# A transformer block on one core: a new order for the head's embedding, three units and the last MLP

## The chip, the core and the metric
## What is computed
Four sequences of 512 tokens pass an embedding, an attention with 32 query heads on 8 key/value heads, and an MLP of 16 small heads. The embedding sums, over 8 shards of the table, the row of a token clipped into the shard. All shards but one give an edge row (their first or last), so the sum is one gathered row plus edge rows with coefficients.
```python
for shard in 8 shards: acc = acc + W[clip(x - start, 0, 1574)]
h = acc + 8 * bias + pos_emb                      # (4, 512, 1024)
a = layernorm(h)
q, k, v = split(a @ w_qkv.T)                      # 32 and 8 and 8 heads of 128
h = h + softmax(causal(q k^T / sqrt(128))) v @ w_dense.T
t = layernorm(h)[..., perm]                       # 16 heads of 64
t = gelu(t @ up[head]) @ down[head]               # 64 -> 256 -> 64
out = h + t[..., unperm]
```

## The kernel before
All work is cut into steps of a kind, a sequence `b`, a group `g` (one key/value head with its four query heads) and an index. `schedule()` lays the steps out in one list from orders written out by hand as strings; every engine walks the same list and does its part of each step. So a token's place in a string is its place in each engine's queue at once. There are a START, then per sequence eight units of about 81 us: unit 0 is FIRST or STATS, unit 1 of later sequences is MLP0, units 2 to 4 MID or MLP, then GATHER, EMBED and TURN, which prepare the next sequence; the last sequence ends with LAST and REST and then the "end" steps, the last sequence's MLP.

The tokens that matter here:
- `A`, `G`, `J`: positions loaded, table rows gathered, and (first sequence) positions added to them. `B0` to `B7`: the edge rows' sum for one half of one block of 128 tokens, with VectorE's statistics. `La`, `Lb`: root of the variance, shift, and ScalarE's normalising of the block. `X0` to `X7`: the normalised block is transposed by TensorE, copied as its high part by ScalarE (L717), and its low part (`xn_lo`, L885) made by VectorE.
- `Q`, `K`, `V`: projections of 24 matmuls in fp32r high/low parts. `S`: scores. `E`: four exponentials on ScalarE; where an order has no `E` token, `unit()` puts the E step directly behind its S. `N`: normalised probabilities, `Ta`/`Tb`: their transposes, `PV`: values, `D`: one of eight dense outputs, added into `hacc` (L830). `H`: the transposed residual. `Z`, `Y`: statistics of the second layernorm and their spreading over partitions. `F`, `P`, `U`, `O`: gather, normalise, up and down projection of a pair of MLP heads, "end F/P/U/O" the same for the last sequence.

Steps of kinds Q, K, V, D, H, Z, Y, B, X, O and end O are jobs. A job writes one of two PSUM banks `fb` in turn, and waits until the job two before it has been read out:
```python
def bank(s):
    return job[s] % 2
def start_job(s):
    if before(s) > 0:
        pe.wait_ge(bank_free[bank(s)], before(s))
```
An X bank is free after L885, a Q bank after L813 (`q_lo`), an H or Y bank after ScalarE's copy (L688, L693), a D bank after L830. Q0 of a new sequence also waits for X7. Weight tiles are loaded four ahead by SyncE (L385), rounded by ScalarE (L633, `split`) and given their low part by GpSimd (L927, `low`); the list `splits` says at which step. Eleven tiles are kept.

At the start VectorE turns the edge rows (0/1 coefficients L748) into three bf16 parts by L762 to L767: one cast and one subtraction of all 96 partitions, then casts and a subtraction of 32.

Of the kernel before, what the change touches and what calls it, by code (L numbers as in the profile page):

```python
# [14 lines left out]
P = 128  # L15
# [34 lines left out]

FIRST = ("S0 N0 Q2 H0 Ta0 H1 Tb0 H2 S1 H3 E1 N1 Q3 H4 Ta1 PV0 Tb1 H5 S2 H6 E2 N2 H7 Q0 Ta2 PV1 Tb2 S3 K N3 Q1 Ta3 PV2 "
         "Tb3 V PV3 VT")
# [3 lines left out]
         "Q1 Ta3 Z5 PV2 Z6 Tb3 V Z7 PV3 VT")  # L57
MLP0 = ("S0 N0 Q2 Y0 Ta0 H0 Y1 Tb0 f H1 S1 H2 E1 N1 Q3 H3 Ta1 D0 Tb1 H4 S2 H5 E2 p F D1 H6 D2 N2 H7 D3 D4 D5 D6 D7 u0 "
        "u1 PV0 u2 u3 Ta2 Q0 Tb2 S3 P N3 PV1 o K U0 U1 Ta3 PV2 U2 U3 Q1 Tb3 V PV3 VT")
# [5 lines left out]
         "PV1 K N3 Q1 Ta3 PV2 Tb3 V PV3 VT")  # L65
TURN = ("S0 N0 Q2 D0 Ta0 La4 D1 Tb0 S1 N1 Lb4 Q3 Ta1 X0 D2 Tb1 X1 S2 D3 D4 N2 X2 D5 X3 D6 X4 D7 X5 PV0 X6 Ta2 X7 Tb2 S3 "
        "PV1 Q0 N3 K Q1 Ta3 PV2 Tb3 V PV3 VT")
LAST = ("S0 N0 Q2 D0 Ta0 D1 Tb0 S1 N1 Q3 W D2 Ta1 PV0 Tb1 S2 D3 D4 N2 D5 Ta2 PV1 Tb2 S3 D6 N3 D7 PV2 Ta3 d0 Tb3 d1 "
        "PV3")
START = ("A G0 G1 G2 G3 J0 J1 J2 J3 B0 B1 La0 B2 Lb0 B3 La1 B4 Lb1 X0 X1 B5 La2 B6 Lb2 X2 X3 B7 La3 Lb3 X4 X5 X6 X7 "  # L70
         "Q0 K Q1 V VT")
# [41 lines left out]
def schedule():  # L113
    steps = unit(START, -1, 7)
    for b in range(B):
        steps += unit(STATS if b else FIRST, b, 0)
        for g in range(1, 5):
            steps += unit((MLP0 if g == 1 else MLP) if b else MID, b, g)
        if b + 1 < B:
            steps += unit(GATHER, b, 5) + unit(EMBED, b, 6) + unit(TURN, b, 7)  # L120
        else:
            steps += [s for s in unit(GATHER, b, 5) if s.kind not in ("A", "G")] + unit(MID, b, 6) + unit(LAST, b, 7)
    steps += unit(REST, B, 0)

    end = lambda kind, i: [Step("end " + kind, B - 1, 0, i)]
    for p in range(PAIRS):
        steps += end("F", p)
    for p in range(PAIRS):
        steps += end("P", p) + end("U", 4 * p) + end("U", 4 * p + 1)
        if p > 0:  # L130
            steps += end("O", p - 1)
        steps += end("U", 4 * p + 2) + end("U", 4 * p + 3)
    return steps + end("O", PAIRS - 1)
# [6 lines left out]
class Tally:  # L140

    def __init__(self):
        jobs = [s for s in STEPS if s.kind in JOBS]
        self.at = {s: n for n, s in enumerate(STEPS)}
# [18 lines left out]
        for m in range(RW):  # L164
            first = Step("X", 0, 0, min(m // 2 * 2 + 1, 7)) if m < 8 else Step("Q", 0, 0, 0)
            self.splits[first].append(m)
# [12 lines left out]
def tower_kernel(nc, x_cols, x_row, table, bias, pos, edge_cols, w_qkv, w_dense, w_mlp, perm_cols, out):  # L179
# [28 lines left out]
    with ctx:  # L208
        def sb(name, shape, dt, at=ctx):
            return at.enter_context(nc.sbuf_tensor(name, shape, dt))  # L210
# [68 lines left out]
        row_sum = sb("row_sum", [P, TT], F32)  # L279
        inv_sum = sb("inv_sum", [P, TT], F32)  # L280

# [28 lines left out]
        gathered = [sem(f"gathered{c}") for c in range(TT)]  # L311
        h_placed = sem("h_placed")
        h_stats = sem("h_stats")
        h_moments = sem("h_moments")
# [46 lines left out]
        def up_bank(s):  # L361
# [3 lines left out]
            return (sc[:, 0, :], sc[:, 1, :], sc[:, 2, :], tp[:, 0, :], tp[:, 1, :], pv[:, :])[s.i % 6]  # L365

        def heads_of(s):

            return (end_at_hi, end_at_lo) if (s.b, s.g) == (B - 1, G - 1) else (at_hi, at_lo)
# [12 lines left out]
        def _(sp):  # L382
# [13 lines left out]
            for part in range(3):  # L396
                at = slice(32 * part, 32 * part + 32)
                sp.dma_start(edge_consts[at, :], edge_cols).then_inc(const_in, 16)
                token_row(at, 0, S, const_in)
            positions(first_pos)  # L400
            for m in range(RAW):
# [31 lines left out]
        def _(pe):  # L433
# [80 lines left out]
            for s in STEPS:  # L514
# [46 lines left out]
                elif s.kind == "H":  # L561
                    half, c = s.i // 4, s.i % 4
                    if s.i == 0:
                        pe.wait_ge(*free(Step("B", s.b, 0, 7)))
                    four(start_job(s), lambda j: h_tok[:, c, (4 * half + j) * P:(4 * half + j + 1) * P])
                elif s.kind == "Z":
# [9 lines left out]
                elif s.kind == "B":  # L576
# [3 lines left out]
                    if s.b == 1 and s.i == 0:  # L580
                        pe.wait_ge(coef_rest, 1)
                    dst = start_job(s)
                    mm = pe.matmul(dst, coef[:, s.b * S + c * P:s.b * S + (c + 1) * P],
                                   edges[:, half * S:(half + 1) * S], start=True, stop=s.b > 0)
                    if s.b == 0:
                        pe.wait_ge(h_placed, c + 1)
                        mm = pe.matmul(dst, ident[:, :], h_tok[:, c, half * S:(half + 1) * S], start=False, stop=True)
                    mm.then_inc(job_full, 1)
                elif s.kind == "X":
# [29 lines left out]
        def _(act):  # L619
# [5 lines left out]
            for part in range(3):  # L625
                at = 32 * part
                act.dma_start(row_buf[at:at + n, :], shards[0:n, VS - 1, :]).then_inc(edge_in, 16)
                act.dma_start(row_buf[at + n:at + 2 * n, :], shards[1:SHARDS, 0, :]).then_inc(edge_in, 16)
                act.dma_start(row_buf[at + 2 * n:at + EDGE, :], bias.partition_broadcast(SHARDS)).then_inc(edge_in, 16)

            def split(m):
# [11 lines left out]
            for s in STEPS:  # L643
# [47 lines left out]
                elif s.kind == "Y":  # L691
                    act.wait_ge(job_full, full(s))
                    act.activation((rstd2 if s.i else mean2)[:, :], fb[:, bank(s), :], copy)\  # L693
                       .then_inc(bank_free[bank(s)], 1)
                elif s.kind == "Z" and s.i == 7:
                    act.wait_ge(stat_step, 6 * s.b + 6)
                    act.activation(root2[:, :], inv_var2[:, :], ACT.Sqrt).then_inc(root_done, 1)
                elif s.kind == "B" and s.b == 0:
                    c, half = s.i // 2, s.i % 2

                    act.wait_ge(h_stats, s.i + 1)
                    act.activation(h_tok[:, c, half * S:(half + 1) * S], fb[:, bank(s), :], copy)\
                       .then_inc(bank_free[bank(s)], 1)
                elif s.kind == "La":
# [3 lines left out]
                elif s.kind == "Lb":  # L708
                    act.wait_ge(shift_done, tally.la[Step("La", *s[1:])] + 1)
                    if s.b == 0:  # L710
                        act.wait_ge(*free(Step("B", 0, 0, 2 * s.i)))
                        act.wait_ge(*free(Step("B", 0, 0, 2 * s.i + 1)))
                    normalise_tokens(s.b, s.i % TT)
# [25 lines left out]
        def _(dve):  # L739
# [30 lines left out]
            for s in STEPS:  # L770
# [85 lines left out]
                elif s.kind == "B":  # L856
                    c, half = s.i // 2, s.i % 2
                    at = h_tok[:, c, half * S:(half + 1) * S]
                    if s.b > 0 and half == 0:
                        dve.wait_ge(gathered[c], 16 * s.b + 16)  # L860
                    dve.wait_ge(job_full, full(s))
                    if s.b > 0:
                        dve.tensor_tensor(at, at, fb[:, bank(s), :], ALU.add).then_inc(bank_free[bank(s)], 1)
                        dve.wait_ge(*free(s))
                    dve.bn_stats(stats[:, c, half, :], at if s.b > 0 else fb[:, bank(s), :]).then_inc(h_stats, 1)
                    if half == 1:
                        dve.wait_ge(h_stats, 8 * s.b + s.i + 1)
                        dve.bn_aggr(moments[:, c, :], stats[:, c, :, :]).then_inc(h_moments, 1)
                elif s.kind == "La":
                    cs = slice(s.i, s.i + 1) if s.i < TT else slice(0, TT)  # L870
# [28 lines left out]
                elif s.kind == "end P":  # L899
                    if s.i == 0:  # L900
                        dve.wait_ge(*free(Step("Y", s.b, 0, 1)))
                        dve.wait_ge(*free(Step("Y", s.b, 0, 0)))
                    at = end_y[:, s.i, :]
                    dve.wait_ge(end_turned[s.i], 16)
                    dve.tensor_tensor(at, end_rows[:, s.i, :], mean2[:, :], ALU.subtract).then_inc(end_centred, 1)
                    dve.wait_ge(end_centred, s.i + 1)
                    dve.tensor_tensor(at, at, rstd2[:, :], ALU.mult).then_inc(end_scaled, 1)
                elif s.kind == "end O":
                    at = end_rows[:, s.i, :]
                    dve.wait_ge(job_full, full(s))  # L910
                    dve.tensor_tensor(at, at, fb[:, bank(s), :], ALU.add).then_inc(bank_free[bank(s)], 1)
                elif s.kind == "O":
                    dve.wait_ge(job_full, full(s))
                    at = hp[:, s.i % 2, :]
                    dve.tensor_tensor(at, at, fb[:, bank(s), :], ALU.add).then_inc(bank_free[bank(s)], 1)

        @block.gpsimd
        def _(pool):
# [11 lines left out]
            for s in STEPS:  # L930
                if s.kind == "G":
# [5 lines left out]
                    else:  # L937
                        pool.wait_ge(pos_in[s.i], 16 * s.b + 16)
                        pool.indirect_dma_start(out=h_tok[:, s.i, :], out_offset=None, in_=table, in_offset=token,
                                                compute_op=ALU.add).then_inc(gathered[s.i], 16)  # L940
                elif s.kind == "J":
                    pool.wait_ge(pos_in[s.i], 16)
                    pool.wait_ge(gathered[s.i], 16)
                    pool.tensor_tensor(h_tok[:, s.i, :], h_tok[:, s.i, :], first_pos[:, s.i, :], ALU.add)\
                        .then_inc(h_placed, 1)
                elif s.kind == "end F":
# [88 lines left out]
```

## Time and profile before

| | |
|---|---|
| median of 3 runs | 2688.78 us (2688.01 to 2689.4) |
| the profiled execution: its own time | 2691.08 us |
| its span, first to last instruction | 2689.3 us |
| mean granted TensorE clock | 0.994 |
| TensorE, VectorE, ScalarE, GpSimd busy | 2603.3, 1247.8, 1233.7, 916.6 us |
| first Q0 starts | 54.84 us |
| last h_tok addition ends | 2679.2 us |

The profile is one execution. "Idle before, releaser" names what ended an engine's wait. Busy time of an engine that others don't wait for costs nothing, and the units between the head and the end repeat with a period of about 81 us.

### The profile page before, as it was taken

The page shows a single profiled execution, that of the slowest core. Times are in us where ns is not written, and L with a number is a line of the kernel's source. Part 1 is how long each engine was busy: PE and PEld are TensorE (multiplying, and loading weights), DVE is VectorE, ACT ScalarE, POOL GpSimd, SP SyncE. Part 2 cuts the span into 40 slices and gives each one's busy share as a digit, 9 for nine tenths or more (in the row PEclk, how much of TensorE's full clock was granted, in tenths as well). Part 3 has the DMA queues.
Part 4 walks back from the last instruction along what each step waited for, and adds up shares of the span by engine and source line. Part 5 has one row for each costly group of instructions (what it writes and reads, how often), then busy time and mean ns, then how long its engine had stood idle before and what let it go on. Part 6 is the DMA issues. An engine that isn't in the chain of part 4 may idle for free.

```text
span 2689.3 us, 35616 instructions
## 1 busy us (share of the span) xinstructions
PE 2603.3 (97%) x12864; PEld 2104.8 (78%) x12864; DVE 1247.8 (46%) x3110; ACT 1233.7 (46%) x3052; POOL 916.6 (34%) x730
## 2 busy tenths in 40 slices
PE   4999999999999999999999999999999999999996
PEld 2788888887877777888887877788888778778872
DVE  4444444454544444455454444446545344434443
ACT  3544444445454454445445454544544444454432
POOL 4333333332333333433233333343332233333312
PEclk8999999999999999999999999999999999999998
DMA  4222223322322222432222222252232222222222
GB/s 126 79 67 75 75 71 109 88 75 59 102 79 82 80 75 87 125 83 63 75 87 80 86 87 78 75 137 66 69 97 72 71 87 87 91 63 75 67 75 71
DMA packets 112129, 221.49 MB, mean 82 GB/s; under 512 B 13394, under 2 KB 13394, under 8 KB 111956
## 3 DMA queue, kind: packets, MB, share of 16 engines
q1 hardware_dynamic: 104400, 193.78, 24.3%
q0 software_dynamic: 7424, 25.17, 3.4%
q8 instruction: 104, 1.70, 0.3%
q14 instruction: 69, 0.57, 0.1%
q10 hardware_dynamic: 132, 0.27, 0.0%
HBM read 202.40 MB, written 16.78 MB: 81 GB/s over the span
## 4 chain that ended last, share of the span: by engine, by line
PE 91%; DVE 4%; ACT 3%; issue 1%; DMA 0%; ACTq 0%; POOL 0%; DVEq 0%
PE fb L435 22%; PE fb L437 21%; PE fb L436 21%; PE tp L456 4%; PE sc L435 2%; PE sc L436 2%; PE sc L437 2%; PE sc L499 2%; PE fb L508 2%; PE pv L435 2%; PE pv L437 2%; PE pv L436 2%; PE sc L447 1%; ACT w_hi L633 1%; PE fb L493 1%; PE pv L468 1%
## 5 line engine op out<-in xcount | busy, mean ns | idle before, releaser
L927 POOL TENSOR_TENSOR w_lo<-w_raw,w_hi 128x512 fp32r<-128x512 f32 x640 | 818.9, 1295 | 1595.2 <-ACT w_hi L633 1595.2
L435 PE MATMUL fb<-xn_hi,w_hi 128*128 128x512 f32 x1536 | 610.8, 398 | 3.4 <-DVE stats L835 1.7
L437 PE MATMUL fb<-xn_hi,w_lo 128*128 128x512 f32 x1536 | 601.6, 392 | 0.0
L436 PE MATMUL fb<-xn_lo,w_hi 128*128 128x512 f32 x1536 | 600.4, 391 | 0.0
L633 ACT ACTIVATE w_hi<-w_raw 128x512 fp32r<-128x512 f32 x640 | 382.6, 632 | 386.7 <-PE fb L437 383.4
L435 PE MATMUL fb<-at_hi,w_hi 128*128 128x512 f32 x992 | 394.8, 398 | 8.2 <-DVE hacc L830 6.1
L649 ACT ACTIVATE prob<-sc,neg_max 128x128 f32<-128x128 f32 (+3 forms) x512 | 262.9, 526 | 280.0 <-DVE neg_max L783 279.1
L437 PE MATMUL fb<-at_hi,w_lo 128*128 128x512 f32 x992 | 387.9, 391 | 0.0
L436 PE MATMUL fb<-at_lo,w_hi 128*128 128x512 f32 x992 | 387.2, 390 | 0.0
L435 PEld LDWEIGHTS fb<-xn_hi,w_hi 128*128 128x128 f32 x1536 | 289.4, 188 | 81.8 <-issue 18.8
L437 PEld LDWEIGHTS fb<-xn_hi,w_lo 128*128 128x128 f32 x1536 | 289.2, 188 | 61.9
L830 DVE TENSOR_TENSOR hacc<-hacc,fb 128x512 f32<-128x512 f32 x256 | 175.8, 687 | 344.7 <-PE fb L437 344.1
L436 PEld LDWEIGHTS fb<-xn_lo,w_hi 128*128 128x128 f32 x1536 | 289.6, 189 | 58.4
L780 DVE CUSTOM_DVE_ANT_0 sc<-sc,mask 128x128 f32<-128x128 f32 (+3 forms) x512 | 235.6, 521 | 1.0 <-PE sc L437 0.6
L791 DVE TENSOR_SCALAR prob<-prob,inv_sum 128x128 f32<-128x128 f32 (+3 forms) x512 | 230.2, 512 | 4.5
L435 PEld LDWEIGHTS fb<-at_hi,w_hi 128*128 128x128 f32 x992 | 186.4, 188 | 58.6 <-issue 22.3
L808 DVE TENSOR_TENSOR at_lo<-pv,at_hi 128x512 fp32r<-128x512 f32 x124 | 85.4, 689 | 287.2 <-ACT at_hi L664 287.2
L437 PEld LDWEIGHTS fb<-at_hi,w_lo 128*128 128x128 f32 x992 | 186.3, 188 | 39.7
L436 PEld LDWEIGHTS fb<-at_lo,w_hi 128*128 128x128 f32 x992 | 186.6, 188 | 36.4
L813 DVE TENSOR_TENSOR q_lo<-fb,q_hi 128x384 fp32r<-128x384 f32 x128 | 71.4, 558 | 299.5 <-ACT q_hi L672 299.0
L671 ACT ACTIVATE q_first<-fb 128x128 f32<-128x128 f32 x128 | 35.4, 277 | 371.9 <-PE fb L437 371.9
L456 PEld LDWEIGHTS tp<-ident,prob 128*128 128x128 f32 x1280 | 150.8, 140 | 62.9 <-issue 18.2
(142 smaller groups left out, 3457.6 us busy)
## 6 DMA issues: line engine op xcount, KB each, us to landing
w_raw<-in_w_qkv SPq DMA_DIRECT2D x384, 256.0 KB, 2.7
w_raw<-in_w_dense SPq DMA_DIRECT2D x256, 256.0 KB, 2.6
h_rows<-hacc SPq DMA_DIRECT2D x32, 256.0 KB, 2.4
h_tok<-in_pos SPq DMA_DIRECT2D x12, 512.0 KB, 6.0
mlp_w<-in_w_mlp SPq DMA_DIRECT2D x24, 256.0 KB, 3.0
first_pos<-in_pos SPq DMA_DIRECT2D x4, 512.0 KB, 10.2
end_w<-in_w_mlp SPq DMA_DIRECT2D x8, 256.0 KB, 4.0
hacc<-in_x_row SPq DMA_DIRECT2D x3, 192.0 KB, 13.9
```

Of the source, the lines that this page charges most:

```text
L435: pe.matmul(dst, a_hi, b_hi, start=first, stop=False)
L436: pe.matmul(dst, a_hi, b_lo, start=False, stop=False)
L437: return pe.matmul(dst, a_lo, b_hi, start=False, stop=last)
L456: return pe.transpose(tp[:, at, c:c + P], prob[:, P_OFF[t] + j * P:P_OFF[t] + (j + 1) * P], ident[:, :])
L633: act.activation(w_hi[:, m % RW, :], w_raw[:, m % RAW, :], copy).then_inc(w_rounded, 1)
L649: act.activation(prob[:, P_OFF[t]:P_OFF[t] + w], sc[:, at, c:c + w], ACT.Exp, bias=neg_max[:, t:t + 1], scale=SCALE, accum_out=row_sum[:, ...
L780: dve.tensor_tensor_reduce(one, one, mask[:, S - w:S], 1.0, LOWEST, ALU.add, ALU.max, row_max[:, t:t + 1]).then_inc(tile_max, 1)
L791: dve.tensor_scalar(at, at, inv_sum[:, t:t + 1], None, ALU.mult).then_inc(prob_ready, 1)
L808: dve.tensor_tensor(lo[:, s.i, :], pv[:, :], hi[:, s.i, :], ALU.subtract).then_inc(pv_free, 1)
L813: dve.tensor_tensor(lo, fb[:, bank(s), at], hi, ALU.subtract).then_inc(bank_free[bank(s)], 1)
L830: dve.tensor_tensor(hacc[:, s.i, :], hacc[:, s.i, :], fb[:, bank(s), :], ALU.add)\
L927: pool.tensor_tensor(w_lo[:, m % RW, :], w_raw[:, m % RAW, :], w_hi[:, m % RW, :], ALU.subtract)\
```

## The change
- Head: SyncE waits for the edge rows before it issues the loads of positions and weights. The positions are added by VectorE (step J), not GpSimd. The first sequence's B steps are no jobs any more: they use six banks that are idle then (`first_bank`), with semaphores of their own, `first_full` and `first_free`. START has a new order with each J in front of its pair of B's, and the first weight tiles are split at B0 to B3 and X1 to X6 in place of the X's and Q0.
- Table loads: ScalarE runs one-column activations (`warm`) with the root's or Gelu's function at the start, at Z0 and after the last root.
- MLP0: the H steps stand earlier. TURN: X2 stands behind S2, X3 to X7 behind D7, around PV0, Ta2, Tb2, S3 and PV1.
- End: `end P` of a pair stands one pair ahead, and the first waits for the two spread statistics one by one.
```diff
-MLP0 = ("S0 N0 Q2 Y0 Ta0 H0 Y1 Tb0 f H1 S1 H2 E1 N1 Q3 H3 Ta1 D0 Tb1 H4 S2 H5 E2 p F D1 H6 D2 N2 H7 D3 D4 D5 D6 D7 u0 "
+MLP0 = ("S0 N0 Q2 Y0 H0 Y1 H1 Ta0 H2 Tb0 f S1 H3 E1 N1 Q3 Ta1 H4 D0 Tb1 H5 S2 H6 H7 E2 p F D1 D2 N2 D3 D4 D5 D6 D7 u0 "
         "u1 PV0 u2 u3 Ta2 Q0 Tb2 S3 P N3 PV1 o K U0 U1 Ta3 PV2 U2 U3 Q1 Tb3 V PV3 VT")
-TURN = ("S0 N0 Q2 D0 Ta0 La4 D1 Tb0 S1 N1 Lb4 Q3 Ta1 X0 D2 Tb1 X1 S2 D3 D4 N2 X2 D5 X3 D6 X4 D7 X5 PV0 X6 Ta2 X7 Tb2 S3 "
-        "PV1 Q0 N3 K Q1 Ta3 PV2 Tb3 V PV3 VT")
+TURN = ("S0 N0 Q2 D0 Ta0 La4 D1 Tb0 S1 N1 Lb4 Q3 Ta1 X0 D2 Tb1 X1 S2 X2 D3 D4 N2 D5 D6 D7 X3 PV0 X4 X5 Ta2 Tb2 S3 X6 "
+        "X7 PV1 Q0 N3 K Q1 Ta3 PV2 Tb3 V PV3 VT")
-START = ("A G0 G1 G2 G3 J0 J1 J2 J3 B0 B1 La0 B2 Lb0 B3 La1 B4 Lb1 X0 X1 B5 La2 B6 Lb2 X2 X3 B7 La3 Lb3 X4 X5 X6 X7 "
+START = ("A G0 G1 G2 G3 J0 B0 B1 J1 La0 B2 B3 Lb0 J2 La1 X0 X1 Lb1 B4 B5 J3 La2 X2 X3 Lb2 B6 B7 La3 X4 X5 Lb3 X6 X7 "
          "Q0 K Q1 V VT")
...
+    steps += end("P", 0)
     for p in range(PAIRS):
-        steps += end("P", p) + end("U", 4 * p) + end("U", 4 * p + 1)
+        if p + 1 < PAIRS:
+            steps += end("P", p + 1)
+        steps += end("U", 4 * p) + end("U", 4 * p + 1)
...
-        jobs = [s for s in STEPS if s.kind in JOBS]
+        jobs = [s for s in STEPS if s.kind in JOBS and s[:2] != ("B", 0)]
...
-            first = Step("X", 0, 0, min(m // 2 * 2 + 1, 7)) if m < 8 else Step("Q", 0, 0, 0)
+            first = Step("B", 0, 0, m) if m < 4 else Step("X", 0, 0, m - 3) if m < 10 else Step("Q", 0, 0, 0)
...
+        def first_bank(i):
+
+            return (sc[:, 0, :], sc[:, 1, :], sc[:, 2, :], tp[:, 0, :], tp[:, 1, :], pv[:, :])[i % 6]
...
+
+            sp.wait_ge(edge_in, 144)
             positions(first_pos)
...
+                    if s.b == 0 and s.i > 5:
+                        pe.wait_ge(first_free, s.i - 5)
+                    dst = start_job(s) if s.b > 0 else first_bank(s.i)
...
+            act.wait_ge(zeroed, 4)
+            act.activation(warm[:, 0:1], ones[:, 0:1], ACT.Sqrt)
...
+                elif s.kind == "Z" and s.i == 0 and s.b == B - 1:
+                    act.activation(warm[:, 1:2], ones[:, 0:1], ACT.Sqrt)
                 elif s.kind == "Z" and s.i == 7:
                     act.wait_ge(stat_step, 6 * s.b + 6)
                     act.activation(root2[:, :], inv_var2[:, :], ACT.Sqrt).then_inc(root_done, 1)
+                    if s.b == B - 1:
+                        act.activation(warm[:, 2:3], ones[:, 0:1], ACT.Gelu)
...
+                elif s.kind == "J":
+                    dve.wait_ge(pos_in[s.i], 16)
+                    dve.wait_ge(gathered[s.i], 16)
+                    dve.tensor_tensor(h_tok[:, s.i, :], h_tok[:, s.i, :], first_pos[:, s.i, :], ALU.add)\
+                       .then_inc(h_placed, 1)
...
                 elif s.kind == "end P":
                     if s.i == 0:
-                        dve.wait_ge(*free(Step("Y", s.b, 0, 1)))
                         dve.wait_ge(*free(Step("Y", s.b, 0, 0)))
                     at = end_y[:, s.i, :]
                     dve.wait_ge(end_turned[s.i], 16)
                     dve.tensor_tensor(at, end_rows[:, s.i, :], mean2[:, :], ALU.subtract).then_inc(end_centred, 1)
+                    if s.i == 0:
+                        dve.wait_ge(*free(Step("Y", s.b, 0, 1)))
...
-                elif s.kind == "J":
-                    pool.wait_ge(pos_in[s.i], 16)
-                    pool.wait_ge(gathered[s.i], 16)
-                    pool.tensor_tensor(h_tok[:, s.i, :], h_tok[:, s.i, :], first_pos[:, s.i, :], ALU.add)\
-                        .then_inc(h_placed, 1)
```

## Rows read from the trace of the kernel before

**Rows 1.** The page: busy us, share of the span, instructions.
```profile
PE 2603.3 (97%) x12864; PEld 2104.8 (78%) x12864; DVE 1247.8 (46%) x3110; ACT 1233.7 (46%) x3052; POOL 916.6 (34%) x730
```
**Rows 2.** TensorE's waits, whole span: us in total, times, longest.
```profile
PE fb L583 <- DVE edges L767: 24.8, 1, 24.8
...
PE sc L499 <- DVE end_y L907: 6.5, 5, 2.2
```
**Rows 3.** Timeline, 11 to 25 us: start, us, engine, line, operation.
```profile
11.14 0.69 DVE L762 CAST edges<-row_buf 96x1024 bf16<-96x1024 f32 x1 [4.20 <-DMA row_buf<-in_bias]
11.87 1.22 DVE L763 TENSOR_TENSOR row_buf<-row_buf,edges 96x1024 f32<-96x1024 f32 x1
12.19 11.87 POOL L944 TENSOR_TENSOR h_tok<-h_tok,first_pos 128x1024 f32<-128x1024 f32 x4 [3.57 <-DMA h_tok<-in_table,rows]
...
18.61 3.24 DVE L766 TENSOR_TENSOR row_buf<-row_buf,edges 32x1024 f32<-32x1024 f32 x1
21.89 2.71 DVE L767 CAST edges<-row_buf 32x1024 bf16<-32x1024 f32 x1
```
**Rows 4.** DMA queues, 2 to 6 us, then 6 to 11.1: packets, MB, share.
```profile
q10 hardware_dynamic: 86, 0.18, 15.7%
...
q1 hardware_dynamic: 266, 0.98, 57.0%
q0 software_dynamic: 156, 0.59, 36.5%
q10 hardware_dynamic: 46, 0.09, 6.1%
```
**Rows 5.** The tile first_pos, its four loads.
```profile
DMA to landing us min/median/max: 7.2/10.2/13.3
```
**Rows 6.** The chain that ended last, in the head: start, us, what.
```profile
25.34 1.71 PE fb L587 x2
27.04 0.43 PE fb L583
...
46.21 0.87 PE fb L587 x2
```
**Rows 7.** Timeline, first matmul of Q0 in the first unit.
```profile
54.84 0.80 PE L435 MATMUL fb<-xn_hi,w_hi 128*128 128x512 f32 x1 [1.41 <-DVE xn_lo L885]
```
**Rows 8.** Windows: us, busy time; the granted clock is third or fourth from the end.
```profile
49.20:51.40 2.20, 0.00 (x0) 0.83 0.63 190
...
54.80:60.90 6.10, 6.06 (x14) 4.79 (x15) 0.00 (x0) 0.30 (x1) 2.37 (x2) 0.50 0.53 145
...
751.90:788.00 36.10, 33.81 (x176) 27.39 (x175) 21.27 (x64) 20.82 (x55) 11.14 (x9) 1.00 0.29 87
```
**Rows 9.** Timeline of the first TURN unit, 617 to 645 us.
```profile
617.14 1.24 ACT L640 ACTIVATE row_buf<-h_tok,shift,rstd 128x1024 f32<-128x1024 f32 x1
618.11 0.39 PE L435 MATMUL fb<-at_hi,w_hi 128*128 128x512 f32 x1
620.03 0.37 ACT L649 ACTIVATE prob<-sc,neg_max 128x128 f32<-128x128 f32 x1 [1.65 <-DVE neg_max L783]
622.05 0.64 ACT L633 ACTIVATE w_hi<-w_raw 128x512 fp32r<-128x512 f32 x1
644.11 0.47 PE L435 MATMUL fb<-xn_hi,w_hi 128*128 128x512 f32 x1
```
**Rows 10.** TensorE's waits, 595 to 660 us.
```profile
PE fb L435 <- DVE hacc L830: 1.2, 3, 0.4
PE tp L456 <- DVE pt_lo L795: 0.7, 1, 0.7
```
**Rows 11.** Timeline of the first MLP0 unit, 757 to 762 us.
```profile
759.69 0.55 DVE L813 TENSOR_TENSOR q_lo<-fb,q_hi 128x384 fp32r<-128x384 f32 x1
759.83 1.09 PE L456 MATMUL tp<-ident,prob 128*128 128x128 f32 x8 [1.29 <-DVE prob L791]
```
**Rows 12.** The chain that ended last, one pair of the last MLP.
```profile
2649.66 0.69 DVE h_tok L911
2650.35 0.61 DVE end_y L905
...
2650.99 0.70 DVE end_y L907
...
2651.73 1.13 PE sc L499 x4
2652.86 1.89 PE fb L508 x8
```

More of the change, by code:

```diff
@@ L280, in tower_kernel @@
         inv_sum = sb("inv_sum", [P, TT], F32)
+        warm = sb("warm", [P, 3], F32)
         with ExitStack() as own:
@@ L312, in tower_kernel @@
         h_placed = sem("h_placed")
+        first_full = sem("first_full")
+        first_free = sem("first_free")
         h_stats = sem("h_stats")
@@ L562, in _ @@
                     half, c = s.i // 4, s.i % 4
-                    if s.i == 0:
+                    if s.i == 0 and s.b > 0:
                         pe.wait_ge(*free(Step("B", s.b, 0, 7)))
+                    elif s.i == 0:
+                        pe.wait_ge(first_free, 8)
                     four(start_job(s), lambda j: h_tok[:, c, (4 * half + j) * P:(4 * half + j + 1) * P])
@@ L581, in _ @@
                         pe.wait_ge(coef_rest, 1)
-                    dst = start_job(s)
+                    if s.b == 0 and s.i > 5:
+                        pe.wait_ge(first_free, s.i - 5)
+                    dst = start_job(s) if s.b > 0 else first_bank(s.i)
                     mm = pe.matmul(dst, coef[:, s.b * S + c * P:s.b * S + (c + 1) * P],
@@ L587, in _ @@
                         mm = pe.matmul(dst, ident[:, :], h_tok[:, c, half * S:(half + 1) * S], start=False, stop=True)
-                    mm.then_inc(job_full, 1)
+                    mm.then_inc(job_full if s.b > 0 else first_full, 1)
                 elif s.kind == "X":
@@ L701, in _ @@
                     act.wait_ge(h_stats, s.i + 1)
-                    act.activation(h_tok[:, c, half * S:(half + 1) * S], fb[:, bank(s), :], copy)\
-                       .then_inc(bank_free[bank(s)], 1)
+                    act.activation(h_tok[:, c, half * S:(half + 1) * S], first_bank(s.i), copy)\
+                       .then_inc(first_free, 1)
                 elif s.kind == "La":
@@ L710, in _ @@
                     if s.b == 0:
-                        act.wait_ge(*free(Step("B", 0, 0, 2 * s.i)))
-                        act.wait_ge(*free(Step("B", 0, 0, 2 * s.i + 1)))
+                        act.wait_ge(first_free, 2 * s.i + 2)
                     normalise_tokens(s.b, s.i % TT)
@@ L860, in _ @@
                         dve.wait_ge(gathered[c], 16 * s.b + 16)
-                    dve.wait_ge(job_full, full(s))
+                    if s.b > 0:
+                        dve.wait_ge(job_full, full(s))
+                    else:
+                        dve.wait_ge(first_full, s.i + 1)
                     if s.b > 0:
@@ L864, in _ @@
                         dve.wait_ge(*free(s))
-                    dve.bn_stats(stats[:, c, half, :], at if s.b > 0 else fb[:, bank(s), :]).then_inc(h_stats, 1)
+                    dve.bn_stats(stats[:, c, half, :], at if s.b > 0 else first_bank(s.i)).then_inc(h_stats, 1)
                     if half == 1:
```

## The prediction
> **What bounds the kernel now.** I read the page's busy times first: TensorE is busy 97% of the span [rows 1]. So a microsecond counts only where TensorE stands still or runs slowly, and the next view was the list of what TensorE waits for [rows 2]: 24.8 us for VectorE's last edge instruction at the head, 6.5 us for `end_y` in the last MLP, and many small waits. The timeline of the head [rows 3] shows what fills the 24.8 us: the edge rows have landed at 11.1, and six VectorE instructions last until 24.6; two casts of one form take 0.69 and 2.71, two subtractions 1.22 and 3.24, the slow ones while GpSimd adds positions. The timelines of one TURN unit [rows 9, 10] and one MLP0 unit [rows 11] show stretches whose order is rewritten, and the chain through the end [rows 12] shows each pair of the last MLP passing through VectorE.
>
> **Head.** The edge queue moved 0.18 MB in the 4 us to 6.0 and 0.09 MB in the 5.1 after it, when other queues moved 1.6 [rows 4]. Without positions the 0.09 MB take some 1.3 us: rows at 7.3, not 11.05 (bounds 7.1 and 11.05). Positions start there. The first landed after 7.2 us beside edges and gathers [rows 5]; I take 5, so 12.3 (bound 14.5). With GpSimd quiet the VectorE chain costs four casts of 0.69, two subtractions of 1.22 and 0.2 of handing over: 5.4, to 12.75 in place of 24.6. The first J, 1.22 by the subtraction's row, ends at 14.0.
>
> From there the list has to be walked, since a J now stands in VectorE's queue between statistics and the next matmul. B0 and B1 at 1.2 GHz take 1.71 and 2.14 [rows 6], full at 17.9. Statistics 0.70, aggregate 0.25, J1 1.22: 20.2, and TensorE idles some 1.8. B3 is full at 22.2 at 2.4 GHz (0.87 and 0.23 a job) or 24.1 at 1.2. ScalarE copies halves (0.60), rounds weight tiles 0 to 3 (0.6 each, which now stand here), takes the root and normalises (1.24 [rows 9]): first block at 25.3 to 27.2. Blocks 2 to 4 follow at 29.5, 35.5 and 40.4 with TensorE fast, each a chain of two copies, two splits, VectorE's low part, a shift and the normalising. X7 is then freed at 43.5. At half clock B4 and B5, X0 and X1, X6 and X7 lie on that chain and add up to 6. The clock was half from 54.8 to 60.9 after 2.2 us without a matmul [rows 8], and the new head is as broken, so I take half of the 6: Q0 starts at 46.8, not 54.84 [rows 7]. The head gives **8.0** (bounds 3 and 11). The warm-up's table load is in this; before it stood on ScalarE between B1 and the first root.
>
> A VectorE instruction with both inputs in SBUF took 2.0 longer beside a GpSimd one [rows 3]. The splits of tiles 0 to 3 run `low` on GpSimd around J1 and J2; 0 to 2 each for J1 and J3 is inside the bounds. The Trainium skill, SBUF — State Buffer, § Who interferes with whom, says that a VectorE instruction with two SBUF inputs and a GpSimd one that reads SBUF exclude each other for a whole instruction. By it, moving J to VectorE turns the exclusion round instead of ending it, and J1 would wait for the rest of one `low`, which makes the head's gain some 7; the trace agrees so far that the slow casts stand exactly beside the GpSimd adds.
>
> **End.** Per pair the chain reads h_tok 0.69, subtract 0.61, scale 0.70, two U 1.13, down 1.89, with gaps 5.11 [rows 12]. With the rows a pair ahead, U 4p needs nothing fresh from VectorE, and TensorE's own work is the period: four U (1.06 and 1.06) and 1.89, about 4.05. ScalarE (four Gelu, 2.0) and VectorE (2.1) fit. Of seven pairs behind the first, six wait today (pair 1's rows are made while pair 0's U run): 6.4. The first subtraction no longer waits for Y1's copy and runs under its matmul: 0.7. The Gelu load lay under VectorE's two instructions already, the root's in idle time: 0. The end gives **7.1** (6 to 8).
>
> **TURN, three times.** Here I expect the loss. X2 is moved directly behind S2. TURN has no E token, so E2 follows S2 in ScalarE's list, and X2's copy stands behind four exponentials that wait for `neg_max`. In the rows S2 ends at 618.11, the exponentials start at 620.03 and the next ScalarE instruction at 622.05 [rows 9]. Copy 0.60 and low part 0.69 free X2's bank at 623.4. Jobs use two banks in turn, and D4 is the second job after X2. X2 itself can run at 618.4 and D3 then ends at 621.65, so D4 waits 1.75. Gone are the waits where an X stood between two D, 1.2 in three [rows 10]. D7 ends at 634.4 with X3 to X7 still to come.
>
> Then X3, PV0 (1.9), X4, X5 and Ta2 end at 638.65. ScalarE behind X3 must normalise twice, copy PV0, X4 and X5, and reaches Ta2's copy at 639.6. VectorE's low part frees the bank at 640.95; until then Tb2 waits, 2.3. S3 ends at 643.05. X6 and X7 run at once, but again their copies stand behind the exponentials of S3: `neg_max` at 644.3, exponentials to 646.4, X7 copied by 647.5, its low part by 648.2. PV1 ends at 645.7, and Q0 must wait 2.6 for X7: it starts at 648.3, before at 644.11 [rows 9]. That is 4.2 a unit with TensorE solid behind it, so nothing gives it back: three units cost **12.6** (bounds 10 and 14).
>
> Two gaps of 2.3 and 2.6 us stand there within 10 us. The granted clock fell to half in the 2.2 us without a matmul up to 51.4, and the 14 matmuls after 54.8 took 6.1 us; at the page's pace of 0.23 they take 3.2: 2.9 lost. In 36.1 us of MLP0 with its gap of 1.29 the clock stayed at full [rows 8]. So the clock costs 0 to 2.9 a unit; the gaps are nearer to the first row, but part of a slow S3 hides in waits. I take 1.6, **4.8** in all.
>
> **MLP0, three times.** Ta0 waits 1.29 for `prob` [rows 11], and H0 is put there. But H0 is the second job after Q2: its bank is freed by `q_lo`, which VectorE does behind N0, at 759.69 + 0.55 = 760.24. So TensorE waits 1.75 in place of 1.29, Ta0 comes after H0, Y1 and H1 at 762.1, and Tb0 waits 0.7 for the low part behind two more ScalarE copies. Q3 starts 1.4 later for like work. Given back are the two bank waits of 0.59 where H6 and H7 stood between D's; 0.1 to 0.3 is new there, since E2 is written behind them. Sum **0** (plus or minus 1.5 for all three). F and P aren't held up: Y1 is full at 761.7, before at 762.1. Stores of `hacc` and weight loads move with their D's by less than 3 us, where the loads run four tiles ahead.
>
> **Sum.** Profiled execution: span 2689.3, its own time 2691.08, of which 1.8 lie around the span. -8.0 - 7.1 + 12.6 + 4.8 + 0 = +2.3, so 2693.4 for that execution. It lies 2.3 above the median of 2688.78, and the median should go to **2691.1**. A difference within 0.2% (5.4 us) can't be told from none in this kernel.
>
> **Rivals.**
> - *The moved X's fill waits and cost nothing.* For it: the waits at their old places are real, 1.9 a unit with Tb2's 0.7. Then the change is -8.0 - 7.1 - 5.6: 2668.1. Against: E2 and E3 stand before those copies in ScalarE's queue. 0.07.
> - *TURN costs its 12.6, but no clock falls there and the head runs fast throughout.* -11 - 7.1 + 12.6: 2683.3. For it: TensorE is nearly solid around the gaps. 0.13.
> - *The clock falls at both gaps of each TURN.* 2 x 2.9 a unit, 17.4 in all: 2688.8 - 2.5 + 17.4 = 2703.7. It ends on the slower side from 2.7 us a unit on. Rows 8 are its support; against it, one stretch at half clock may cover both gaps. 0.25.
> - *The head doesn't gain as walked, because J and the early splits hold the chain.* Head 3: 2696.1 with the 4.8. 0.07.
> - *Forecast*: 0.48, own range 2684 to 2697, with a tenth of it beyond 0.2% on either side.
>
> Slower: 0.25 + 0.04 + 0.05 = 0.34. Faster: 0.07 + 0.06 + 0.05 = 0.18. Same: 0.48. The range 2682 to 2700 leaves out the first rival and the upper part of the third.
>
> **What would show it.** Edge rows landed near 7.3, casts at 0.69 and subtractions at 1.22, Q0 of the first unit between 43.5 and 50. In the TURN units a wait of D4 on `xn_lo` near 1.8 and of Q0 on `xn_lo` near 2.6, and a granted clock under 1.00 there. In MLP0 a wait of an H on `q_lo` of 1.7. At the end no `end_y` wait after the first, and 4.05 between h_tok rows. I am wrong if TensorE's list has no wait on `xn_lo` beyond the head, or if X2's bank is freed before 622.

## The result and the profile after

The changed kernel takes 2695.06 us (median of 13 runs, 2693.73 to 2698.11), the kernel before 2688.78 in the same runs: ratio 1.0024, 95% interval 1.0016 to 1.0031. It is slower by 6.3 us. The profiled execution has a span of 2695.1 us, 5.8 more than before. In one of the later comparisons a single execution of the kernel before took 14861 us; the ratios leave it out.

TensorE's waits over the whole span come first, in the columns of [rows 2]:
```profile
PE sc L600 <- DVE edges L791: 15.7, 1, 15.7
PE tp L469 <- DVE pt_lo L819: 15.7, 25, 2.2
PE fb L448 <- DVE xn_lo L917: 13.3, 7, 2.5
...
PE sc L512 <- DVE end_y L940: 1.5, 1, 1.5
```
The 24.8 us at the head are 15.7 now, and `end_y` has one wait left. Two rows are new in size: 13.3 us for `xn_lo`, six of the seven waits far behind the head, and 15.7 for `pt_lo`. So the list already names the place of the loss. The 9.1 us that the longest wait of the head gave up are not all gained: the other waits up to Q0 were 3.2, 2.3, 2.3, 1.4 and 0.7 us before, and are these now:
```profile
PE fb L506 <- ACT row_buf L661: 5.0, 2, 3.1
PE fb L506 <- ACT prob L661: 4.7, 2, 3.6
PE sc L604 <- DVE h_tok L899: 3.1, 2, 1.8
PE fb L448 <- DVE xn_lo L917: 1.6, 1, 1.6
```
That is 14.4 in place of 9.9, which leaves the 4.6 by which Q0 starts earlier.

The offset between the two traces, read at instructions that both have, gives the sum. The marks are the start of the first Q0, of the variance step in each TURN unit, of the root behind each sequence, of the last dense addition, and the span.

| mark | before | after | after less before | stretch that lies between |
|---|---|---|---|---|
| first Q0 | 54.84 | 50.28 | -4.56 | |
| variance, TURN 1 | 601.69 | 596.22 | -5.47 | head: **-5.5** |
| root, sequence 0 | 750.71 | 749.81 | -0.90 | TURN 1: **+4.6** |
| variance, TURN 2 | 1254.18 | 1253.99 | -0.19 | MLP0: **+0.7** |
| root, sequence 1 | 1403.19 | 1410.68 | +7.49 | TURN 2: **+7.7** |
| variance, TURN 3 | 1906.78 | 1914.93 | +8.15 | MLP0: **+0.7** |
| root, sequence 2 | 2055.82 | 2069.26 | +13.44 | TURN 3: **+5.3** |
| last addition to hacc | 2626.31 | 2640.32 | +14.01 | MLP0: **+0.6** |
| span | 2689.3 | 2695.1 | +5.8 | end: **-8.2** |

TURN 17.5, MLP0 1.9, head -5.5, end -8.2. A stretch called MLP0 also holds the units behind MLP0 up to the next mark, whose orders are the same in both kernels.

Head, timeline (answers to [rows 3] and [rows 7]):
```profile
10.22 0.69 DVE L786 CAST edges<-row_buf 96x1024 bf16<-96x1024 f32 x1 [3.44 <-DMA row_buf<-in_bias]
...
12.20 0.68 DVE L788 CAST edges<-row_buf 32x1024 bf16<-32x1024 f32 x1
...
13.64 1.22 DVE L790 TENSOR_TENSOR row_buf<-row_buf,edges 32x1024 f32<-32x1024 f32 x1
...
16.35 1.23 DVE L899 TENSOR_TENSOR h_tok<-h_tok,first_pos 128x1024 f32<-128x1024 f32 x1 [0.78 <-DMA first_pos<-in_pos]
...
50.28 0.80 PE L448 MATMUL fb<-xn_hi,w_hi 128*128 128x512 f32 x1 [1.56 <-DVE xn_lo L917]
```
The casts of 32 partitions took 0.68 in place of 2.71 and the subtraction 1.22 in place of 3.24, so the chain of six is 5.35 us, 10.22 to 15.57. It begins at 10.2, though, and J0 then waits another 0.78 for its positions.

TURN 1 on ScalarE and TensorE (two timelines, in the order of the list; answer to [rows 9]):
```profile
614.56 0.37 ACT L670 ACTIVATE prob<-sc,neg_max 128x128 f32<-128x128 f32 x1 [1.64 <-DVE neg_max L807]
...
616.59 0.60 ACT L741 ACTIVATE xn_hi<-fb 128x512 fp32r<-128x512 f32 x1
...
641.16 1.10 ACT L741 ACTIVATE xn_hi<-fb 128x512 fp32r<-128x512 f32 x2
```
```profile
618.06 0.47 PE L448 MATMUL fb<-at_hi,w_hi 128*128 128x512 f32 x1 [1.67 <-DVE xn_lo L917]
635.70 0.44 PE L469 MATMUL tp<-ident,prob 128*128 128x128 f32 x2 [2.20 <-DVE pt_lo L819]
643.14 0.50 PE L448 MATMUL fb<-xn_hi,w_hi 128*128 128x512 f32 x1 [2.53 <-DVE xn_lo L917]
```
X2's copy (L741) starts as the exponentials of E2 end, and D4 starts at 618.06 after 1.67 us of standing. Tb2 stands for 2.20, until the low part of Ta2's transposes is made behind the copies of X4 and X5. Q0 stands for 2.53, until the copies of X6 and X7 have come through behind E3. The three waits stand in all three units alike; only the third unit's last one is shorter, 1.7.

The granted clock in TURN 2. First the two later waits there, then windows of 4 us: length, TensorE's busy time with its instructions, the granted clock, and DMA share and GB/s.
```profile
1293.47 0.69 PE L469 MATMUL tp<-ident,prob 128*128 128x128 f32 x2 [2.20 <-DVE pt_lo L819]
1302.44 0.50 PE L448 MATMUL fb<-xn_hi,w_hi 128*128 128x512 f32 x1 [2.53 <-DVE xn_lo L917]
```
```profile
1290.00:1294.00 4.00, 1.80 (x15) 0.93 0.21 65
1294.00:1298.00 4.00, 4.00 (x21) 0.64 0.02 4
1298.00:1302.00 4.00, 1.91 (x13) 1.00 0.00 0
1302.00:1306.00 4.00, 3.56 (x11) 0.71 0.00 0
1306.00:1310.00 4.00, 4.00 (x17) 0.86 0.00 0
```
After each of the two gaps the clock goes to its half level (a share under 1.00 is a window partly at that level) and comes back. That unit lost 7.7 us. TURN 1 kept the full clock throughout and lost 4.6. TURN 3 had one fall, behind its gap of 2.2 (0.70 and 0.87 over 1954 to 1962), and lost 5.3.

MLP0, TensorE's waits from 745 to 785 us (answers to [rows 11]):
```profile
PE fb L506 <- DVE q_lo L837: 1.9, 1, 1.9
PE tp L469 <- DVE pt_lo L819: 0.6, 1, 0.6
PE fb L448 <- ACT hacc L709: 0.3, 1, 0.3
```
That is 2.8 us. Before, the waits of this unit were 2.2 (from 745 to 840 us, the rest of the unit):
```profile
PE tp L456 <- DVE prob L791: 1.3, 1, 1.3
PE fb L435 <- DVE hacc L830: 0.9, 2, 0.4
```
The end, one pair of the chain (answers to [rows 12]):
```profile
2669.67 1.48 PE sc L512 x5
2671.16 0.42 PE sc L512
2671.59 1.87 PE fb L521 x8
2673.45 0.62 PE tp L512
```
VectorE has left the chain of the pairs, and a pair takes 3.78 us, 2669.67 to 2673.45, in place of 5.11.

### The profile page after: what moved, and what is told of

It is laid out like the page before. It is cut to its first block, busy times and chain, and to the rows that moved or that the text cites. A ratio compares the mean times of both kernels' runs of the same rounds, so it can differ in the third digit from the quotient of the medians.

```text
span 2695.1 us, 35616 instructions
## 1 busy us (share of the span) xinstructions
PE 2605.4 (97%) x12864; PEld 2107.5 (78%) x12864; DVE 1245.3 (46%) x3114; ACT 1233.5 (46%) x3054; POOL 906.5 (34%) x726
## 4 chain that ended last, share of the span: by engine, by line
PE 90%; ACT 4%; DVE 4%; issue 1%; DMA 0%; ACTq 0%; POOL 0%; DVEq 0%
PE fb L448 22%; PE fb L450 21%; PE fb L449 21%; PE tp L469 4%; PE sc L512 2%; PE sc L448 2%; PE sc L449 2%; PE sc L450 2%; PE fb L521 2%; PE pv L448 2%; PE pv L450 2%; PE pv L449 2%; ACT w_hi L654 1%; PE sc L460 1%; ACT prob L670 1%; PE fb L506 1%
## 5 line engine op out<-in xcount | busy, mean ns | idle before, releaser
L448 PE MATMUL fb<-xn_hi,w_hi 128*128 128x512 f32 x1536 | 610.4, 397 | 10.2 <-DVE xn_lo L917 8.3
L450 PE MATMUL fb<-xn_hi,w_lo 128*128 128x512 f32 x1536 | 601.4, 392 | 0.0
L449 PE MATMUL fb<-xn_lo,w_hi 128*128 128x512 f32 x1536 | 599.9, 391 | 0.0
L469 PE MATMUL tp<-ident,prob 128*128 128x128 f32 x1280 | 184.5, 275 | 16.1 <-DVE pt_lo L819 15.7
```

Of the source, the lines that this page charges most:

```text
L448: pe.matmul(dst, a_hi, b_hi, start=first, stop=False)
L449: pe.matmul(dst, a_hi, b_lo, start=False, stop=False)
L450: return pe.matmul(dst, a_lo, b_hi, start=False, stop=last)
L469: return pe.transpose(tp[:, at, c:c + P], prob[:, P_OFF[t] + j * P:P_OFF[t] + (j + 1) * P], ident[:, :])
```

## The experiments

**TURN's old order in the changed kernel.**
```diff
-TURN = ("... X1 S2 X2 D3 D4 N2 D5 D6 D7 X3 PV0 X4 X5 Ta2 Tb2 S3 X6 X7 PV1 ...")
+TURN = ("... X1 S2 D3 D4 N2 X2 D5 X3 D6 X4 D7 X5 PV0 X6 Ta2 X7 Tb2 S3 PV1 ...")
```

> The changed kernel with TURN's old order, all else as changed. Theory A (moved X's in TURN hold two banks behind the exponentials: 4.2 us a unit, plus what the clock loses in the gaps): the changed kernel's 2695.1 less 12.6 to 17.7, so 2677 to 2682; TensorE's only waits on xn_lo beyond the head gone, three hacc waits of 0.3 to 0.4 a unit back. Theory B (TURN costs at most its visible change of waits, and the missing gain is in the head and in MLP0): 2690 or more.

Measured: 2679.92 (6 runs), ratio to before 0.9966 (0.9954 to 0.9979). That is 15.1 us under the changed kernel: theory A, in the middle of its span. With this one line back the change is a gain, and each TURN stretch is 149.1 us long, as before (149.0).

**TURN's new order alone.** The same line, the other way round, in the kernel before.

> The kernel before with only TURN's new order. Theory A: 2688.8 plus 12.6 to 17.7, so 2701 to 2706, waits of 1.7, 2.2 and 2.5 us in each TURN unit, and a granted clock under 1.00 behind some of them. Theory B: 2693 or less.

Measured: 2706.39 (4 runs), ratio 1.0065 (1.0048 to 1.0082), 17.3 us above before. The first unit shows `xn_lo` 4.2 in two waits and `pt_lo` 2.2, the changed kernel's own numbers, so neither depends on the rest of the change. All three units show a fall of the clock in the profiled execution, and the TURN stretches are 7.7, 6.2 and 6.1 longer than before. That execution was the slowest of the four, 2712.25.

**Copies ahead of the exponentials.** TURN keeps its new places for X, but E2 and E3 are written out behind them, which moves only ScalarE's work.
```diff
-TURN = ("... X1 S2 X2 D3 D4 N2 ... Tb2 S3 X6 X7 PV1 ...")
+TURN = ("... X1 S2 X2 E2 D3 D4 N2 ... Tb2 S3 X6 X7 E3 PV1 ...")
```

> The changed kernel, TURN's new places for X kept on every engine, but with E2 written behind X2 and E3 behind X7, so that ScalarE copies them before its exponentials. Theory A (ScalarE's queue order is the cause): D4 and Q0 no longer wait for xn_lo, the wait of 2.2 before Tb2 stays, Q0 comes where it came before; 2677 to 2683. Rival (the new places are bad in themselves: banks and transposes in a row, or VectorE's load): the waits stay above 1 us each and the time stays above 2688.

Measured: 2681.10 (7 runs), ratio 0.9969 (0.9957 to 0.9980). TensorE's waits from 590 to 650 us:
```profile
PE tp L469 <- DVE pt_lo L819: 2.2, 1, 2.2
PE fb L448 <- DVE q_lo L837: 0.6, 1, 0.6
PE fb L506 <- ACT row_buf L661: 0.3, 2, 0.2
```
The 4.2 us for `xn_lo` are gone, the 2.2 before Tb2 stay. X2's copy and the first exponential in ScalarE's timeline:
```profile
615.56 0.60 ACT L741 ACTIVATE xn_hi<-fb 128x512 fp32r<-128x512 f32 x1 [0.75 <-PE fb L506]
616.46 0.37 ACT L670 ACTIVATE prob<-sc,neg_max 128x128 f32<-128x128 f32 x1 [0.30 <-DVE neg_max L807]
```
The copy fits into time in which ScalarE stood waiting for `neg_max` anyway. Two `E` tokens in a string are worth 14 us here. Against the old order at 2679.9 the times show neither gain nor loss in the new places for X, since the intervals overlap. The trace shows that the gap of 2.2 before Tb2, which stays, isn't free: the TURN stretches are 148.9, 150.4 and 150.5 us against 149.0 before. The first kept the full clock; in the other two it fell behind that gap (0.64 in the 4 us that hold its end, 1288 to 1292), for 1.4 each. Both `E` tokens were moved together, so their shares are told apart by the waits alone.

**MLP0's old order in the changed kernel.**

> The changed kernel with MLP0's old order. The two profiles put 0.5 to 0.7 us a unit on the new order: 2695.1 less 1.8, so 2693.3. If MLP0's new order were a gain as walked by its own removed waits (1.29 and two of 0.43), 2697 or more. Prediction on record said 0 plus or minus 1.5.

Measured: 2694.03 (10 runs), ratio 1.0019 (1.0009 to 1.0029). 1.0 us under the changed kernel agrees with the 1.9 of the table in sign, but the two intervals overlap, so the times alone don't show it. The stretches do, as the table at the end of this section shows.

**Head and end alone** (both old orders back).

> The changed kernel with both old orders, TURN's and MLP0's: what head, table loads and end give by themselves. The profiles say -5.5 and -8.2, so 2689.1 less 13.7 gives 2675.4; with the run that had only TURN's old order at 2679.9 and MLP0's new order worth 0.6 a unit, 2678. My walk on record (-8.0 and -7.1) gives 2674.

Measured: 2677.73 (4 runs), ratio 0.9955 (0.9937 to 0.9973). This is where the run with TURN's old order and 0.6 us a unit for MLP0 had put it (2678). The table loads of the `warm` activations are in it, and no run takes them out of the head.

**The end alone**, in the kernel before.
```diff
+    steps += end("P", 0)
     for p in range(PAIRS):
-        steps += end("P", p) + end("U", 4 * p) + end("U", 4 * p + 1)
+        if p + 1 < PAIRS:
+            steps += end("P", p + 1)
+        steps += end("U", 4 * p) + end("U", 4 * p + 1)
```

> The kernel before with the end's change alone (rows a pair ahead, the first waits one by one; no table loads moved). My walk on record: -7.1. The two profiles together: -8.2. So 2680.6 to 2681.7; the h_tok additions 3.8 to 4.1 us apart, where they were 5.11.

Measured: 2678.86 (5 runs), ratio 0.9968 (0.9954 to 0.9981): 8.9 us under before in its own comparison. The pairs stand 3.78 us apart. No `warm` activation is in this kernel, and its first U starts 0.14 us behind VectorE's scaling, as in the kernel before and in the changed one; so moving Gelu's table load gave the end nothing. Between this ratio and the one with the head (0.9955) lie 0.0013, 3.5 us for the head, with intervals that overlap. The profiles give the head by a mark: the variance step of TURN 1 starts at 601.7, 602.5 and 599.9 in the three kernels with the old head, and between 594.6 and 598.7 in the six that have the changed kernel's head (the changed kernel itself, the one with TURN's old order, copies first, MLP0's old order, head and end alone, mixed orders). The means, 601.4 and 596.8, are 4.6 apart.

**Gathers held back.** In the kernel with head and end alone, GpSimd waits for the edge rows before the four gathers.
```diff
+            pool.wait_ge(edge_in, 144)
             for s in STEPS:
                 if s.kind == "G":
```

> Head and end changed, and GpSimd also waits for the edge rows before it issues the four gathers. The edge rows landed at 10.1 us, not at 7.3 as I had it. If the gathers' traffic holds them (they moved 0.95 MB between 6 and 10 us), they now land at 7 to 8, and J0 comes later, for the gathers start late: Q0 at 50 or later. If the edge queue is slow by itself, they still land at about 10.

```profile
7.04 0.69 DVE L786 CAST edges<-row_buf 96x1024 bf16<-96x1024 f32 x1 [0.60 <-DMA row_buf<-in_bias]
...
11.76 0.69 DVE L791 CAST edges<-row_buf 32x1024 bf16<-32x1024 f32 x1
15.64 1.23 DVE L899 TENSOR_TENSOR h_tok<-h_tok,first_pos 128x1024 f32<-128x1024 f32 x1 [3.20 <-DMA h_tok<-in_table,rows]
```
One run: the rows are there at 7.0, where the seven traces that differ from it in this stage by the four gathers alone have 9.2 to 10.2. So it was the gathers' traffic. The chain is done at 12.45, and VectorE then waits 3.20 us for the gather that was held. Q0 starts at 49.47, total 2676.60, inside the range of the kernel without the hold (2675.03 to 2678.90): the wait has moved.

**The edge wait of SyncE left out** (one run, head and end alone otherwise).
```diff
-            sp.wait_ge(edge_in, 144)
             positions(first_pos)
```

> Head and end changed, without SyncE's wait for the edge rows, so positions are issued at 4 us as before the change. If that wait is what brings the edge rows forward, they land at 11 again and J0 starts at about 16.5; if it only delays the positions, J0 starts near 16 or earlier and Q0 is not later than the 48.5 to 50.5 of its neighbours. Casts stay at 0.69 in either case, for GpSimd adds nothing.

The first cast starts at 11.58, J0 at 16.97 without a wait, Q0 at 51.16, total 2677.98. SyncE's wait brings the edge rows forward by 1.4 to 2.3 us (9.24 to 10.22 in the seven traces with it), but J0 only from 16.97 to between 16.1 and 16.5, since the positions are later. It is worth under 1 us of J0, and neither Q0 nor the total lies outside what the kernels with it show.

**J on GpSimd again** (one run, head and end alone otherwise), at its new places in the list.
```diff
-                    dve.tensor_tensor(h_tok[:, s.i, :], h_tok[:, s.i, :], first_pos[:, s.i, :], ALU.add)\
+                    pool.tensor_tensor(h_tok[:, s.i, :], h_tok[:, s.i, :], first_pos[:, s.i, :], ALU.add)\
```

> Head and end changed, but the positions are added by GpSimd again, at J's new places. If the exclusion of the two engines made the slow casts, the casts and subtractions keep 0.69 and 1.22 only if J0 starts behind them, which it does (positions land at 16 us); J0 to J3 cost about 2.5 to 3 us in place of 1.22 on the path of B0, B2 and B6: Q0 some 4 us later than 50.3. If VectorE's queue was the bound in the head, Q0 is not later.

```profile
PE sc L600 <- DVE edges L791: 14.7, 1, 14.7
PE sc L604 <- POOL h_tok L972: 8.9, 2, 5.4
```
Each J takes 2.34 to 2.36 us on GpSimd, and B2 waits 5.4 for the second one, behind the splits in GpSimd's queue. Q0 starts at 54.12. In the same kernel with J on VectorE it started at 48.53, but that is the earliest of six traces with the changed head (48.5 to 52.1, mean 50.5), so J's engine costs some 3.6 us, near the 4 that were expected. With it the head is nearly back where the three traces with the old one are (54.5 to 55.6): by this single run most of the head's gain hangs on J. What the six banks and the new START order give was not tried alone. The total, 2678.10, doesn't show the loss. From the last addition to `hacc` on, this execution took 50.9 us against 53.8, with a better clock there (0.96 against 0.92 over 2600 to 2690 us).

**Staged loads.** The first block's positions and gather go at once, the other three behind the edge rows.
```diff
+            sp.dma_start(first_pos[:, 0, :], pos[0:P, :]).then_inc(pos_in[0], 16)
             sp.wait_ge(edge_in, 144)
...
                     pool.wait_ge(rows_ready, 1)
+                    if s.b == 0 and s.i == 1:
+                        pool.wait_ge(edge_in, 144)
```

> Head and end changed, with the first block's positions and gather issued at once and the other three only behind the edge rows. If the gathers' traffic was what I had missed and the rest of my walk holds (32.8 us from J0's end to Q0), the edge rows land near 7.5, J0 starts at 12.9 and Q0 at 46.8, some 3 us under the head of the changed kernel: 2675 where the same kernel without staging had 2677.7. If J1's gather is late instead, Q0 stays at 49 to 50 and the time at 2677 to 2678.

Measured: 2677.06 (4 runs), ratio 0.9961 (0.9946 to 0.9976). The first cast starts at 11.27, later than without staging, J0 at 16.66 and Q0 at 50.87. So one gather and one block of positions can hold the edge rows as much as all four gathers do (the other kernel with this staging, the last one below, has 10.27 and 15.66, still far from the 7.0 without gathers). My repair was wrong, and the term in the walk can't be had this way.

**Mixed orders.** Head and end as changed; MLP0's old beginning with its new second half, and X2 of TURN between S2 and E2.
```diff
+MLP0 = ("S0 N0 Q2 Y0 Ta0 H0 Y1 Tb0 f H1 S1 H2 E1 N1 Q3 H3 Ta1 H4 D0 Tb1 H5 S2 H6 H7 E2 p F D1 D2 N2 D3 D4 ...")
+TURN = ("... X1 S2 X2 E2 D3 D4 N2 D5 X3 D6 X4 D7 X5 PV0 X6 Ta2 X7 Tb2 S3 PV1 ...")
```

> As the run before this one, with MLP0's old beginning (Ta0 ahead of H0) and its new second half (H6 and H7 between S2 and E2), and X2 of TURN between S2 and E2, the other X's at their old places. The queue theory: two bank waits of 0.43 a MLP0 unit become one of 0.3, one of 0.43 a TURN unit goes, no wait on xn_lo: 1 to 3 us under the run before it. If X behind S2 were bad in itself: at or over it.

Measured: 2675.71 (4 runs), ratio 0.9945 (0.9927 to 0.9963), 2.0 us under head and end alone. The intervals overlap, so this is the direction expected and no more. The stretches below give 1.0 of it to MLP0 and nothing to X2's new place.

**Both together,** the mixed orders and the staged loads.

> The staged loads with the mixed orders of TURN and MLP0: the two gains add, 2672.5 to 2674, against 2675.7 without staging; at or above 2675.7 if the staging only moves the wait.

Measured: 2677.36 (5 runs), ratio 0.9958 (0.9944 to 0.9971). No better. The lowest median is that of the mixed orders without staging: 14.8 us under the kernel before in its own comparison, and by the two ratios some 21 under the changed one. The intervals of the four versions near it overlap with its own.

**The stretches in all traces.** The marks of the first table, read in all fourteen kernels, tell the orders apart more sharply than the times:

| stretch | order | length, us |
|---|---|---|
| TURN | old (eight kernels) or X2 alone moved, behind it E2 (two) | 148.9 to 149.1 |
| TURN | new (three kernels) | 153.5 to 156.7 |
| TURN | new, copies first | 148.9, 150.4, 150.5 |
| MLP0 to the next variance step, first two | old (nine kernels) | 503.5 to 503.7 |
| the same | new (three) | 504.1 to 504.3 |
| the same | mixed (two) | 503.2 to 503.3 |
| end | old (two) | 63.0, 63.2 |
| end | new (twelve) | 50.9 to 55.2, mean 53.7 |

So MLP0's new order costs 0.6 us a unit, and its mixed one gives 0.3. The end varies with the clock: its first four U take 2.90 us in the changed kernel and 1.52 in the kernel with the end alone.

## Why the prediction was right, and where it was off

The forecast was 2691.1, likeliest within 0.2% and leaning to slower. Measured were 2695.06 and 0.24%, just beyond that line and inside the range: not the outcome held likeliest, but the next. For the profiled execution the sum said +2.3 and the trace says +5.8. The head is off by 2.5, MLP0 by 1.9, the end by -1.1, TURN by 0.1.

- **TURN**, the deciding step, held in place, cause and size. Waits of 1.75, 2.3 and 2.6 were walked; 1.67, 2.20 and 2.53 stand in the trace. 12.6 plus 4.8 for the clock were forecast, and 17.5 measured. Copies ahead of the exponentials removed the two `xn_lo` waits of the three and left the one for `pt_lo`, which shows the cause of the two: the place of an E in ScalarE's queue. That D4's wait reaches TensorE through the two banks used in turn is read from the code and the trace; no run changed the banks.
- **The clock.** 0 to 2.9 a unit, 1.6 taken: the three units exceed 4.2 by 0.4, 3.5 and 1.1. That they add up to 5.0 against 4.8 is partly luck, for 3.5 lies outside the bound of a unit. Over the nine new TURN units of three traces the excess is 0.3 to 3.5, in the mean 1.7. In TURN 2 that a fall came behind both gaps is in the windows. The rival with falls at both gaps of every unit held for one unit of three. What decides between units was not tried.
- **The end**: -7.1 forecast, -8.2 and -8.9 measured, and -9.4 as the difference of the means in the table above. The mis-sized term is the period: 4.05, of which I took the U's from a chain in which each pair of them restarted after a wait. Running on, four U and a down projection take 3.78. Six periods of 5.11 less 3.78 are 8.0, in place of 6.4, and 0.7 for the first wait comes to them; the rest goes with the clock of the execution, which the sum for the end had left out (the first four U alone differ by 1.4).
- **The head**: -8.0 forecast, -5.5 in the profile, 4.6 as a mean over several. The step that failed is the landing of the edge rows, 7.3 forecast, 10.2 measured. I had put their delay on the positions' traffic alone, from a row in which both other queues were moving data; with the gathers held, they land at 7.0. From J0's end to Q0 I had walked 32.8 us, and the trace has 32.7 (17.58 to 50.28). That close a hit is luck: the same code took 31.2 to 34.4 in the other traces with this head, with the clock at its half level in different places. J0's positions took 6.0 where I took 5.
- **MLP0**: 0 plus or minus 1.5 forecast, +1.9, just outside. Each new wait came about as walked (`q_lo` 1.9 for 1.75, `pt_lo` 0.6 for 0.7, `hacc` 0.3). The mis-sized term is what was given back: the two bank waits were 0.43 each, not 0.59. With 2.8 us of waits in place of 2.2 the unit loses 0.6; the walk's own terms came to 0.1 to 0.3 and were rounded to 0.
- VectorE beside GpSimd: with GpSimd quiet the casts were at 0.68 and the subtractions at 1.22. The kernel with the end alone keeps the old head, and there GpSimd's additions are over at 23.3:
```profile
12.07 11.25 POOL L948 TENSOR_TENSOR h_tok<-h_tok,first_pos 128x1024 f32<-128x1024 f32 x4 [3.21 <-DMA h_tok<-in_table,rows]
...
21.16 3.24 DVE L769 TENSOR_TENSOR row_buf<-row_buf,edges 32x1024 f32<-32x1024 f32 x1
24.44 0.69 DVE L770 CAST edges<-row_buf 32x1024 bf16<-32x1024 f32 x1
```
Its last cast took 0.69 where two of the same form, beside the additions, took 2.71. For the subtraction, which has two SBUF inputs, the Trainium skill's rule on the two engines (SBUF — State Buffer, § Who interferes with whom) is borne out by that: 1.22 without GpSimd, 3.24 beside it. In the run with head and end alone one J took 2.31 us where the others took 1.23 and 1.28:
```profile
22.47 1.28 DVE L899 TENSOR_TENSOR h_tok<-h_tok,first_pos 128x1024 f32<-128x1024 f32 x1
26.93 2.31 DVE L899 TENSOR_TENSOR h_tok<-h_tok,first_pos 128x1024 f32<-128x1024 f32 x1
```
```profile
26.90 3.48 POOL L960 TENSOR_TENSOR w_lo<-w_raw,w_hi 128x512 fp32r<-128x512 f32 x2 [2.02 <-ACT w_hi L654]
```
A `low` starts 0.03 us ahead of it, and the two `low`s of that line take 3.48 where two take 2.50 elsewhere. That they were the reason is argued from this; no run took them away.

## What to carry to other kernels

When one list orders all engines, moving a step moves it in every queue: follow its buffer to the instruction that frees it, and look at what stands ahead of that one in its own queue. Here transposes were moved to places that TensorE could serve, and their 0.6 us copies to bad ones for ScalarE, and two order tokens separated 2695 from 2681. Walking the list by hand with durations of the old trace gave each new wait of TURN and MLP0 to 0.2 us as long as the clock was full; what it missed most was a transfer, whose time depends on everything that moves beside it.

## What the runs showed of the hardware

- A stall costs more than its length when it brings the clock down: 4.6 us for a unit of TURN at full clock, 7.7 for the same instructions with two falls, and 4.5 to 7.7 over nine such units. With a single long gap in the unit, 2.2 us, the clock fell in two units of three, for 1.4 each.
- Less than 0.3 MB of edge rows landed at 7.0 us with positions and gathers held back, at 9.2 to 10.2 beside four gathers, at 11.1 to 11.7 beside both, and at 10.3 and 11.3 beside one gather and one block of positions.
- The same addition of 128x1024 f32 took 2.34 us on GpSimd with VectorE free, 2.94 beside VectorE's casts (median before), and 1.23 on VectorE.
